# State-space products woven between the projections, with the kernel sums moved ahead

## The chip, the cores and the metric

The kernel runs on one core of a Trainium2 chip. The metric is the device time of one execution, in microseconds (us). The kernel before takes 555.73 us, the median of three runs (555.17 to 556.35). Its one profiled execution took 551.41 us.

The engines are named as in the profile: PE (TensorE, matmul), DVE (VectorE), ACT (ScalarE), POOL (GpSimd) and SP (SyncE, which here only issues DMAs). PSUM has eight banks of 128 x 512 floats, called `bank[0]` to `bank[7]` in the code.

## The reference

Images and text tokens are embedded to h of 32 samples x 68 positions x 256 features. Then come a gated state-space layer (`attn`) and a mixture of four experts with top-2 routing (`ffn`), each added to h. The change lies in the state-space layer:

```python
u = x @ W_x.T + b_x                                  # x: layer norm of h; 512 channels
g = sigmoid(x @ W_g.T + b_g)
u = u * g + conv3(u) * (1 - g)                       # width 3, each channel by itself
dt = clip(softplus(x @ W_dt.T + b_dt).mean(axis=(0, 1)), 0.001, 2.0)      # one number a channel
A = -softplus(A_raw);  A_d = exp(A * dt[:, None]);  B_d = (A_d - 1) / (A + 1e-6) * B_ssm
# scan over the 68 positions: state = A_d * state + B_d * u_t;  y_t = sum_s state * C_ssm
out = y @ W_out.T + b_out
h = h + layernorm(x + out) * ln_g + ln_b
```

Since A_d and B_d don't depend on the position, the scan is a causal convolution: y_t = sum over s of K[t-s] u_s, with a kernel K[k] = sum over the 16 states of B_d C A_d^k, one for each channel. The program computes it that way: for each channel a 68 x 68 Toeplitz matrix of K times the 68 x 32 matrix of u (positions x samples).

## The kernel before, in words

Every engine runs its own instruction list in order, and semaphores join them. The stages that matter:

**A (to about 70 us).** Embedding, layer norm, transposed x (`xT_hi`, `xT_lo`), transposed weights (`WT`). Each projection is done in three matmuls of split parts (hi x hi, hi x lo, lo x hi) by `split3` (lines 392 to 394).

**dt (about 70 to 102 us).** Twenty blocks of x @ W_dt, whose softplus goes from PE to DVE to ACT and back to DVE; DVE then computes `adt` = A * dt (L1279).

**C (about 102 to 189 us), ordered by the list `C_STEPS`.** `("proj", j)` is one chunk of 128 channels, j = 0 to 3. It goes over `NB` = 5 blocks of columns (four of 512, one of 128); a block is 12 matmuls on PE (six for u, six for g), three passes on ACT (`ur` L397, `hb` L1034, `gb` L1041) and four on DVE (L1323 to L1326, which build the mixed u in `hb`). `("turn", j)` transposes the mixed chunk on PE, four samples to a step (L811), through a ring of PSUM banks 4 to 7, and ACT (for the last chunk ACT and DVE in turn) copies it to `U2` (L427). The kernels K are made in between: POOL multiplies the exponents (`Eb`, L596), ACT takes the exponential (L1051), and `kernel_sum(j)` on DVE weighs and sums them (L1309, L1311). `KERNEL_SUMS` puts these sums behind `turn 0`, `turn 1` and the second block of chunk 3. `("kernels",)`, ahead of turn 2, transposes K (L804); DVE copies it to `kt` (L1336, L1338), and SP stores it to `ssm_kernels` (`kpd`) in DRAM (L483).

**Products (about 189 to 251 us).** SP loads the Toeplitz matrices of 32 channels at a time, 16 loads of 680 KB each into three buffers `Tb` (L497; a load waits until the products that read its buffer are done). Load q serves two product steps v = 2q and 2q + 1 of 16 matmuls each (L851; the trace has two records for each matmul), in four column groups of 32 samples. ACT copies the even steps' result to `y` (L966) and DVE the odd ones (L1346), through PSUM banks 0 to 3. In load q, each of the four chunks has eight channels, so all four chunks must be turned before the first product. Beside this SP loads the experts' first weights (`w1raw`, four loads of 512 KB, L503), ACT and DVE split them (`w_hi` L966, `w_lo` L1351), and PE transposes the router's and the output's weights (`BEHIND`, `weights(q)`).

**D (from about 251 us).** Tile by tile: y is transposed (L868), multiplied by `Wo` (L874), added to the residual (L1383), normed, routed (L1428 to L1463) and scattered to the experts' lists; from about 325 us the experts' blocks run beside it, then the combination. The order in D is a sort of steps by the due times in `STARTS` and `AT` (`order(who)`).

Of the kernel before, what the change touches and what calls it, by code (L numbers as in the profile page):

```python
# [23 lines left out]
ALU = mybir.AluOpType  # L24
# [5 lines left out]
def build_kernel(nc, ins, out):  # L30
# [36 lines left out]
    with stack:  # L67
# [66 lines left out]
        ong_b = sb("ong_b", [P, D])  # L134
        onb_b = sb("onb_b", [P, D])
# [22 lines left out]
        def place(start, end, *wanted):  # L158
# [12 lines left out]
        R5 = R4 + size(H * B)  # L171
# [6 lines left out]
        y = at("y", [P, H // HC, L], R1)  # L178
# [15 lines left out]
        ur, hb, gb0 = place(R3, R4, ("ur", [P, 2, N + 2 * B]), ("hb", [P, 2, N]), ("gb0", [P, N]))  # L194
# [4 lines left out]
        (U2,) = place(R4, R5, ("U2", [L, HC, H // HC, B]))  # L199
        h1, x2s, yT, r1, h0r, xb, xg, bT_hi, bT_lo, hn = place(  # L200
            R4, R5, ("h1", [P, NT, D]), ("x2s", [P, NT, DX]), ("yT", [P, 2, HC, P]),
            ("r1", [P, 4, D]), ("h0r", [P, 4, D]), ("xb", [P, 3, D]), ("xg", [P, 4, DX]), ("bT_hi", [P, 2, DC, P], F32R),
            ("bT_lo", [P, 2, DC, P], F32R), ("hn", [P, 2, HF]))
        got_a, got_b, acc = place(R1, R2, ("got_a", [P, 4, D]), ("got_b", [P, 4, D]), ("acc", [P, 4, D]))
# [15 lines left out]
        (kt,) = place(R6, TOP, ("kt", [LR, QN, HC, QH]))  # L220

        (Wor1,) = place(R6, TOP, ("Wor1", [P, H]))
        Wor = [Wor0, Wor1]
# [63 lines left out]
        for k in range(NT + 3):  # L287
# [4 lines left out]
            if k in (NT, NT + 1):  # L292
# [24 lines left out]
                rs=14.6, b3=27.1, c1w=-31.4, c1s=26.7),  # L317
# [3 lines left out]
                table=50.0, rel=47.7, wts=134.7, b1=-14.6, b2=-3.4, rs=4.5, b4=32.1, c1=-1.9, c2=22.3),  # L321
            "odd": dict(yT=21.1, xb=8.8, out=17.5, h0in=6.5, x2T=4.3, lgm=8.1, scat=-0.8, gat=18.4, fin=0.3)}

        def place_of(who, kind, i):

            if kind in BLOCKWISE:
# [9 lines left out]
        def order(who):  # L336

            steps = []
            for kind in AT[who]:
                count = NK if kind in BLOCKWISE else NT if kind in BY_TILE else 2 if kind in BY_PART else len(FB)  # L340
# [4 lines left out]
        C_STEPS = [("proj", 0), ("proj", 1), ("turn", 0), ("proj", 2), ("turn", 1), ("proj", 3), ("kernels",), ("turn", 2),  # L345
                   ("turn", 3)]


        KERNEL_SUMS = {("turn", 0): [0], ("turn", 1): [1, 2], (3, 1): [3]}
# [6 lines left out]
        C_RING = []  # L356
        for step in C_STEPS:
            if step[0] == "kernels":
                C_RING.append(("kT",))
            if step[0] == "turn":  # L360
                C_RING += [("uT", step[1], k) for k in range(B // 4)]

        def c_reader(q):

            if C_RING[q][0] != "uT":
                return "dve"
            _, j, k = C_RING[q]
            return "act" if j < HC - 1 or k % 2 == 0 else "dve"
# [4 lines left out]


        G_RING = [("rw",), ("cbc",), ("wo", 0), ("wo", 1)]

        BEHIND = {15: [0], 19: [1], 29: [2, 3]}
# [40 lines left out]
        def turned(eng, j, who):  # L418

            for k in range(B // 4):  # L420
                q = C_RING.index(("uT", j, k))
                if c_reader(q) != who:
# [1155 lines left out]
```

## Time and profile before

| | |
|---|---|
| median of the runs | 555.73 us |
| profiled execution, its time | 551.41 us |
| profiled execution, its span (first to last instruction) | 549.7 us |
| granted TensorE clock, mean | 0.88 |
| busy: PE / DVE / ACT / POOL | 425.8 / 349.5 / 292.8 / 170.2 us |

The span leaves out 1.71 us of the profiled execution's own time. The page gives busy time as an average over stages with different limits; where a row below has a stretch, that stretch alone is meant. Rows of the timeline read: start, duration, engine, line, operation, output<-input, shapes, and in brackets the idle time ahead of it with what ended it.

### The profile page before, as it was taken

What the parts mean: (1) busy time and instruction counts of PE and PEld (TensorE: products, weight loads), DVE (VectorE), ACT (ScalarE), POOL (GpSimd) and SP (SyncE); (2) the same over time, 40 slices, a digit from 0 to 9 for tenths busy, and PEclk for the clock granted to TensorE, in tenths of its full rate; (3) what the DMA queues carried; (4) which work ended last, traced back from release to release, by engine and by line L of the source; (5) the groups of instructions that cost most, each with busy time, mean ns of one, the idle gap of its engine ahead of it and who ended that gap; (6) DMA issues with size and microseconds to landing.
All of it is one profiled execution on the core that took longest, in us unless ns stands there. A gap on an engine that the chain in (4) does not pass through costs nothing.

```text
span 549.7 us, 10131 instructions
## 1 busy us (share of the span) xinstructions
PE 425.8 (77%) x3078; PEld 352.2 (64%) x3078; DVE 349.5 (64%) x1071; ACT 292.8 (53%) x655; POOL 170.2 (31%) x368
## 2 busy tenths in 40 slices
PE   4999989499893854757888759999897999999100
PEld 2789866388682743646676547878776888887100
DVE  6866578889899200323678876796674466565464
ACT  3754368388982410312543434776674777878121
POOL 2000000500000000001245585577777755655100
PEclk9999999889997765558988969999998999999755
DMA  8961210000000799985111142222224233332342
GB/s 177 217 174 35 63 15 0 1 0 2 0 1 0 173 253 221 202 174 186 47 58 59 58 119 75 59 74 92 79 77 116 69 97 97 98 114 98 124 130 72
DMA packets 51616, 50.97 MB, mean 93 GB/s; under 512 B 25672, under 2 KB 46188, under 8 KB 50156
## 3 DMA queue, kind: packets, MB, share of 16 engines
q1 hardware_dynamic: 47116, 39.70, 30.0%
q0 software_dynamic: 3552, 9.74, 4.8%
q10 hardware_dynamic: 896, 0.89, 0.5%
q8 instruction: 26, 0.43, 0.4%
q14 instruction: 26, 0.21, 0.1%
HBM read 35.56 MB, written 15.81 MB: 93 GB/s over the span
## 4 chain that ended last, share of the span: by engine, by line
PE 44%; DMA 16%; DVE 15%; issue 8%; POOL 8%; ACT 6%; SPq 2%; POOLq 0%; DVEq 0%; ACTq 0%
DMA Tb<-ssm_kernels 9%; PE bank L953 9%; PE bank L392 6%; PE bank L394 5%; PE bank L393 5%; PE bank L874 4%; DMA got_b<-expert_y 3%; POOL expert_y L682 2%; PE bank L851 2%; POOL sorted_x L640 2%; PE bank L943 2%; PE bank L868 1%; DVE hb L1324 1%; PE bank L925 1%; DVE hb L1323 1%
## 5 line engine op out<-in xcount | busy, mean ns | idle before, releaser
L953 PE MATMUL bank<-w,hr 128*128 x320 | 77.9, 387 | 4.4 <-DVE ysb L1535 4.3
L953 PEld LDWEIGHTS bank<-w,hr 128*128 128x128 f32 x320 | 58.8, 194 | 12.6 <-issue 6.0
L1131 ACT ACTIVATE hr<-bank,gsel 128x128 f32<-128x128 f32 x160 | 60.0, 458 | 12.4 <-PE bank L943 12.4
L682 POOL DMA_INDIRECT expert_y<-ysb,toid x40 | 43.4, 1085 | 35.6 <-DVE ysb L1535 24.8
L851 PE MATMUL bank<-Tb,U 68*32 68x68 f32 x1024 | 33.9, 298 | 26.0 <-DMA Tb<-ssm_kernels 24.3
L851 PEld LDWEIGHTS bank<-Tb,U 68*32 68x32 f32 x1024 | 29.4, 144 | 30.1 <-DMA Tb<-ssm_kernels 27.6
L640 POOL DMA_INDIRECT sorted_x<-x2s,slot x34 | 33.5, 986 | 31.1 <-DVE slot L1463 22.6
L874 PE MATMUL bank<-Wo,yT 128*128 128x256 f32 x136 | 38.5, 434 | 2.5 <-ACT yT L966 2.3
L1346 DVE COPY y<-bank 128x272 f32<-128x272 f32 x16 | 7.1, 442 | 50.2 <-PE bank L851 50.2
L1123 ACT ACTIVATE hn<-bank,nmrh,rsh 128x512 f32<-128x512 f32 x40 | 31.1, 777 | 14.5 <-DVE nmrh L1529 12.3
L596 POOL TENSOR_TENSOR Eb<-adt,kio 128x1088 f32<-128x1088 f32 x4 | 8.0, 2027 | 98.4 <-DVE adt L1279 98.4
L1535 DVE COPY ysb<-bank 128x256 f32<-128x256 f32 x40 | 16.9, 421 | 33.4 <-PE bank L953 29.8
L392 PE MATMUL bank<-w_hi,bT_hi 128*128 x80 | 35.0, 437 | 1.5 <-ACT hn L1123 0.8
L616 POOL MEMSET ones<- 2x128 f32 x1 | 0.2, 194 | 110.2 <-PE bank L835 110.2
L966 ACT ACTIVATE y<-bank 128x272 f32<-128x272 f32 x16 | 6.4, 397 | 52.1 <-PE bank L851 52.1
L1520 DVE BATCH_NORM_STATS2 bsth<-bank 128x6 f32<-128x512 f32 x40 | 27.8, 694 | 9.4 <-PE bank L394 9.1
L874 PEld LDWEIGHTS bank<-Wo,yT 128*128 128x128 f32 x136 | 28.4, 220 | 7.4 <-ACT yT L966 3.5
L394 PE MATMUL bank<-w_hi,bT_lo 128*128 x80 | 31.6, 394 | 0.0
L393 PE MATMUL bank<-w_lo,bT_hi 128*128 x80 | 31.3, 391 | 0.0
L943 PE MATMUL bank<-ident,hn 128*128 128x128 f32 x160 | 24.4, 275 | 0.0
L966 ACT ACTIVATE bT_hi<-bank 128x256 fp32r<-128x256 f32 x40 | 15.3, 383 | 16.5 <-PE bank L925 16.2
L427 ACT ACTIVATE U<-bank 68x512 f32<-68x512 f32 x28 | 15.1, 598 | 15.2 <-PE bank L811 15.1
(290 smaller groups left out, 1188.1 us busy)
## 6 DMA issues: line engine op xcount, KB each, us to landing
Tb<-ssm_kernels SPq DMA_DIRECT2D x16, 680.0 KB, 9.4
xg<-sorted_x SPq DMA_DIRECT2D x40, 129.0 KB, 2.1
XI<-in_x_dram SPq DMA_DIRECT2D x12, 288.0 KB, 5.7
h0r<-h_spill SPq DMA_DIRECT2D x17, 128.0 KB, 2.2
got_a<-expert_y SPq DMA_DIRECT2D x17, 128.0 KB, 2.8
got_b<-expert_y SPq DMA_DIRECT2D x17, 128.0 KB, 4.7
out_dram<-acc SPq DMA_DIRECT2D x17, 128.0 KB
w1raw<-in_L_ffn_w_dram SPq DMA_DIRECT2D x4, 512.0 KB, 11.1
```

The lines of the kernel that those rows point to most:

```text
L392: pe.matmul(out_ap, a_hi, b_hi, start=start, stop=False)
L393: pe.matmul(out_ap, a_hi, b_lo, start=False, stop=False)
L394: return pe.matmul(out_ap, a_lo, b_hi, start=False, stop=stop)
L640: pool.indirect_dma_start(xsd[p], bass.IndirectOffsetOnAxis(ap=slot[:, i, n:n + 1], axis=0), x2s[:, i, :], None).then_inc(sem("scattered") ...
L682: pool.indirect_dma_start(yd, bass.IndirectOffsetOnAxis(ap=toid[:, i % 8:i % 8 + 1], axis=0), ysb[:, i % 2, :], None).then_inc(sem(f"y_sto ...
L851: mm = pe.matmul(bank[v % 4][j * B:(j + 1) * B, k * L:(k + 1) * L], U2[:, j, hq, :], Tb[q % 3][0:L, :, j * QH + hq % QH], start=True, stop ...
L874: pe.matmul(ps, yT[:, i % 2, j, :], Wo[:, j, :], start=(j == 0), stop=False)
L943: mm = pe.transpose(bank[3 + i % 2][:, c * P:(c + 1) * P], hn[:, i % 2, c * P:(c + 1) * P], ident[:])
L953: mm = pe.matmul(bank[6][:, 0:D], hr[:, i % 3, c, :], w2[:, bass.ds(expert[i], 1), c, :].rearrange("p o n -> p (o n)"), start=(c == 0), st ...
L1123: act.activation(hn[:, i % 2, :], bank[1 + i % 2][:], ACT.Identity, scale=rsh[:, i % 2:i % 2 + 1], bias=nmrh[:, i % 2:i % 2 + 1]).then_inc ...
L1131: last = act.activation(hr[:, i % 3, c, :], bank[3 + i % 2][:, c * P:(c + 1) * P], ACT.Relu, scale=gsel[:, i, 0, c:c + 1], bias=gsel[:, i, ...
L1520: link(dve.bn_stats(bsth[:, i % 2], bank[1 + i % 2][:]))
```

## The change

- `C_STEPS` is written per column block: `("proj", j, nb)`. The four kernel sums come first on DVE, ahead of all mixing; the transposed kernels (`kT`) follow chunk 0 on PE. Behind chunk 1 and the turn of chunk 0, `woven(2)` and `woven(3)` put two product steps behind each of the first four blocks of chunks 2 and 3. Each product step now needs one chunk only: load q holds 32 neighbouring channels (`quads`), so loads 0 to 3 serve chunk 0, 4 to 7 chunk 1, and so on. The turn of chunk 3 stands between the products of chunk 2 and those of chunk 3.
- The turns' ring has two banks (4, 5) read by ACT and DVE in turn, for every chunk; the products' results have two (6, 7).
- DVE makes the exponents of chunks 0 and 1, POOL those of 2 and 3. Small constants are computed inside the dt loop, at `q == CONSTS_AT` (8).
- One gate buffer `gb` in place of two; `U2` holds two chunks, not four. SBUF is laid out anew.
- `w1raw`, the last norms' vectors and `w2` are loaded from ACT's queue near the end of the products; splitting w1 is a step `w1s` of stage D on ACT and DVE.

```diff
-        KERNEL_SUMS = {("turn", 0): [0], ("turn", 1): [1, 2], (3, 1): [3]}
+        CONSTS_AT = 8
+        SV = 2 * QN // HC
+        turns = lambda j: [("uT", j, k) for k in range(B // 4)]
+        woven = lambda j: [s for nb in range(NB) for s in [("proj", j, nb)] + [
+            ("ssm", SV * (j - 2) + v) for v in range(2 * nb, min(2 * nb + 2, SV))]]
+        C_STEPS = ([("proj", 0, nb) for nb in range(NB)] + [("kT",)] + [("proj", 1, nb) for nb in range(NB)] + turns(0) + [("rw",)]
+                   + woven(2) + turns(1) + [("cbc",)] + woven(3) + turns(2) + [("wo", 0), ("wo", 1)]
+                   + [("ssm", v) for v in range(2 * SV, 3 * SV)] + turns(3) + [("ssm", v) for v in range(3 * SV, 4 * SV)])
...
             for q in range(QN):
                 if q == 0:
                     sp.wait_ge(sem("kernel_sum"), HC)
-                if q == 2:
-                    sp.wait_ge(sem("mixed"), HC * NB)
                 if q >= 3:
                     sp.wait_ge(sem("ssm_mm"), 2 * (q - 2))
...
-            for j in range(HC):
+            for j in range(2, HC):
                 pool.tensor_tensor(Eb[:, j], adt[:, j].rearrange("p (o s) -> p o s", o=1).broadcast_to([P, L, S]),
...
+                if step[0] == "ssm":
+                    v = step[1]
+                    q, j, r = v // 2, v // SV, v % SV
+                    if v % SV == 0:
+                        for who in ("act", "dve"):
+                            last = max(k for k, s in enumerate(C_RING) if s[0:2] == ("uT", j) and c_reader(k) == who)
+                            pe.wait_ge(sem(f"c_read_{who}"), c_read(last)[1])
+                    pe.wait_ge(sem(f"toep_in{q % 3}"), 16 * (q // 3 + 1))
+                    if v >= 2:
+                        pe.wait_ge(sem("y_dve" if v % 2 else "y_act"), (v - 2) // 2 + 1)
...
+                ring = C_RING.index(step)
+                if ring >= 2:
+                    who, n = c_read(ring - 2)
+                    pe.wait_ge(sem(f"c_read_{who}"), n)
+                ps = bank[4 + ring % 2]
...
+            act.wait_ge(sem("conv_consts"), 5)
+            u_parts(0, 0)
+            for j in range(HC):
+                act.wait_ge(sem("exponent" if j < 2 else "exponent_pool"), j % 2 + 1)
+                act.activation(Eb[:, j], Eb[:, j], ACT.Exp).then_inc(sem("powers"), 1)
+                if j == 1:
+                    u_parts(0, 1)
...
+                    if v == 4 * SV - 4:
+                        act.wait_ge(sem("g_mm"), HC * NB)
+                        for e in range(E):
+                            act.dma_start(w1raw[:, e], ins["L0_ffn_w1"][e].rearrange("(c p) h -> p c h", p=P)).then_inc(
+                                sem("experts_in"), 16)
...
+            for j in range(2):
+                dve.tensor_tensor(Eb[:, j], adt[:, j].rearrange("p (o s) -> p o s", o=1).broadcast_to([P, L, S]),
...
+            for j in range(HC):
+                kernel_sum(j)
             for step in C_STEPS:
...
+                elif kind == "w1s":
+                    dve.wait_ge(sem("w1_hi"), i + 1)
+                    dve.tensor_tensor(w1_lo[:, i], w1raw[:, i], w1_hi[:, i].bitcast(F32), ALU.subtract).then_inc(
+                        sem("w1_split"), 1)
```

DVE's list right behind `adt`, in the program before (`nmr`, `nbg`, `ncw`, `vb` are small constants, `hb` rows are the mixing):

```order
L1283 SCALAR_TENSOR_TENSOR nmr<-mv,rs 128x17
L1286 TENSOR_SCALAR nbg<-vec 128x4
L1287 TENSOR_SCALAR ncw<-cw 128x12
L1288 TENSOR_SCALAR ncw<-cw 128x4
L1290 TENSOR_TENSOR vb<-vec,ncw 128x4
L1291 TENSOR_TENSOR vb<-vb,vec 128x4
L1295 MEMSET ur 128x2x32 x2
L1323 SCALAR_TENSOR_TENSOR hb<-ur,ncw,hb 128x480
```

The same place of DVE's list in the changed program (the pair of L1300 and L1302 stands there four times):

```order
L1279 TENSOR_TENSOR adt<-amat,dt 128x64
L1287 TENSOR_TENSOR Eb<-adt,kio 128x1088 x2
L1296 SCALAR_TENSOR_TENSOR wmix<-wmix,winv 128x64
L1297 TENSOR_TENSOR wmix<-wmix,bcs 128x64
L1298 TENSOR_TENSOR wmix<-wmix,bcs 128x64
L1300 TENSOR_TENSOR Eb<-Eb,wmix 128x1088
L1302 TENSOR_REDUCE Kk<-Eb 128x68
```

The two exponents and the four sums have moved ahead of the first mixing row, and the constants have gone from there.

PE's list at the end of stage C and the start of the products, in the program before:

```order
L394 MATMUL bank<-xT_hi,WTg_lo 128x128
L804 MATMUL bank<-ident,Kk 68x128 x4
L811 MATMUL bank<-ident,hb 68x128 x64
L851 MATMUL bank<-Tb_119,U_92 32x68 x32
L851 MATMUL bank<-Tb_120,U_92 32x68 x32
L851 MATMUL bank<-Tb_121,U_92 32x68 x32
```

PE's list in the changed program, from the first block of chunk 2 to the second (the last rows of the one, the product row of 32 matmuls, the first rows of the other):

```order
L384 MATMUL bank<-xT_lo,WTg_hi 128x512
L385 MATMUL bank<-xT_hi,WTg_lo 128x512
L786 MATMUL bank<-Tb_122,U_54 32x68 x32
L383 MATMUL bank<-xT_hi,WTx_hi 128x512
L384 MATMUL bank<-xT_lo,WTx_hi 128x512
```

Where all products stood behind the last turn, each of the first four blocks of chunks 2 and 3 is now followed by the 32 matmuls of one load; eight rows of products are left behind `turn 2`.

DVE's list in stage D of the changed program, at the first `w1s` step:

```order
L1441 TENSOR_REDUCE x2s<-gt 128x2
L1442 CAST slot<-sl 128x2x2
L1495 TENSOR_TENSOR w_lo<-w1raw,w_hi 128x1024
L1375 RECIPROCAL rs<-sd 128x2
L1376 SCALAR_TENSOR_TENSOR r_100<-r_100,mv,lng_b 128x256
```

In the program before, `slot` is followed at once by the reciprocal; the other three `w_lo` rows stand at the same place of the next three pairs of tiles.

## Rows read from the trace of the kernel before

**Rows 1.** The page: what the chain that ended last consists of.

```profile
DMA Tb<-ssm_kernels 9%; PE bank L953 9%; PE bank L392 6%; PE bank L394 5%; PE bank L393 5%; PE bank L874 4%; DMA got_b<-expert_y 3%; POOL expert_y L682 2%; PE bank L851 2%; POOL sorted_x L640 2%; PE bank L943 2%; PE bank L868 1%; DVE hb L1324 1%; PE bank L925 1%; DVE hb L1323 1%
```

**Rows 2.** One stretch: length, busy time (instructions) of each engine, PE clock, DMA, GB/s.

```profile
190.00:220.00 30.00, 15.68 (x488) 13.64 (x477) 3.09 (x7) 3.18 (x8) 0.00 (x0) 0.59 1.02 235
```

**Rows 3.** Timeline of PE, the products of three of the 16 loads.

```profile
189.01 2.07 PE L851 MATMUL bank<-Tb,U 68*32 68x68 f32 x64 [0.98 <-DVE U L427]
...
221.19 2.10 PE L851 MATMUL bank<-Tb,U 68*32 68x68 f32 x64 [0.87 <-DMA Tb<-ssm_kernels]
224.50 2.09 PE L851 MATMUL bank<-Tb,U 68*32 68x68 f32 x64 [1.21 <-DMA Tb<-ssm_kernels]
```

**Rows 4.** The tile Tb: shortest, median and longest time from issue to landing.

```profile
DMA to landing us min/median/max: 6.1/9.4/13.5
```

**Rows 5.** Timeline of DVE behind the dt loop, and of POOL beside it.

```profile
101.95 0.23 DVE L1279 TENSOR_TENSOR adt<-amat,dt 128x64 f32<-128x64 f32 x1
102.25 0.17 DVE L1287 TENSOR_SCALAR ncw<-cw 128x12 f32<-128x12 f32 x1
102.46 1.89 DVE L1288 TENSOR_SCALAR ncw<-cw 128x4 f32<-128x4 f32 x1
104.49 1.84 DVE L1290 TENSOR_TENSOR vb<-vec,ncw 128x4 f32<-128x4 f32 x1
102.27 8.02 POOL L596 TENSOR_TENSOR Eb<-adt,kio 128x1088 f32<-128x1088 f32 x4 [98.42 <-DVE adt L1279]
```

**Rows 6.** Timeline of DVE: a block's mixing starts, chunk 1 ends, and one kernel sum.

```profile
111.95 0.72 DVE L1323 SCALAR_TENSOR_TENSOR hb<-ur,ncw,hb 128x480 f32<-128x480 f32 x1 [3.49 <-ACT gb L1041]
114.73 0.74 DVE L1323 SCALAR_TENSOR_TENSOR hb<-ur,ncw,hb 128x512 f32<-128x512 f32 x1
117.63 0.74 DVE L1323 SCALAR_TENSOR_TENSOR hb<-ur,ncw,hb 128x512 f32<-128x512 f32 x1
137.73 0.33 DVE L1326 TENSOR_TENSOR hb<-ur,hb 128x160 f32<-128x160 f32 x1
157.22 1.28 DVE L1309 TENSOR_TENSOR Eb<-Eb,wmix 128x1088 f32<-128x1088 f32 x1
159.74 1.28 DVE L1309 TENSOR_TENSOR Eb<-Eb,wmix 128x1088 f32<-128x1088 f32 x1
```

**Rows 7.** Timeline of PE: matmuls of a block at half and at full clock, one turn.

```profile
110.92 0.63 PE L394 MATMUL bank<-xT_hi,WTx_lo 128*128 128x512 f32 x1
111.35 0.63 PE L392 MATMUL bank<-xT_hi,WTx_hi 128*128 128x512 f32 x1
114.69 0.40 PE L393 MATMUL bank<-xT_lo,WTx_hi 128*128 128x512 f32 x1
114.92 0.39 PE L394 MATMUL bank<-xT_hi,WTx_lo 128*128 128x512 f32 x1
149.78 3.68 PE L811 MATMUL bank<-ident,hb 128*68 128x128 f32 x32
```

**Rows 8.** Timeline of DVE: copies of the turn and of y.

```profile
187.20 0.69 DVE L427 COPY U<-bank 68x512 f32<-68x512 f32 x1 [0.18 <-PE bank L811]
251.03 0.44 DVE L1346 COPY y<-bank 128x272 f32<-128x272 f32 x1 [3.48 <-PE bank L851]
```

**Rows 9.** Stretches (columns as rows 2) of products alone, for PE's clock.

```profile
189.00:191.00 2.00, 1.99 (x64) 1.80 (x64) 0.00 (x0) 0.40 (x1) 0.00 (x0) 1.00 0.99 226
193.00:196.00 3.00, 2.20 (x76) 1.87 (x68) 0.44 (x1) 0.40 (x1) 0.00 (x0) 0.92 1.12 291
225.00:230.00 5.00, 4.63 (x124) 4.10 (x116) 1.66 (x3) 2.37 (x4) 0.00 (x0) 0.50 1.01 216
```

**Rows 10.** Timeline of DVE: splitting w1, and a wait in stage D.

```profile
244.28 1.21 DVE L1351 TENSOR_TENSOR w_lo<-w1raw,w_hi 128x1024 fp32r<-128x1024 f32 x1
285.15 0.42 DVE L1383 TENSOR_TENSOR r<-bank,xb 128x256 f32<-128x256 f32 x1 [1.32 <-PE bank L878]
```

**Rows 11.** The tile h0r (the residual, read back in stage D): time to landing.

```profile
DMA to landing us min/median/max: 1.9/2.2/3.3
```

More of the change, by code:

```diff
@@ L354, in reached @@
             return max(0, n0 - lag * B), (N if nb == NB - 1 else n0 + w - lag * B)
[L356 to L361, printed above, removed]
         def c_reader(q):
[L365 to L368, printed above, removed]
+            kind = C_RING[q][0]
+            return "act" if kind == "wo" or (kind == "uT" and C_RING[q][2] % 2 == 0) else "dve"
         def c_read(q):
@@ new lines, in _ @@
+                    _, j, nb = step
+                    n0, w = BLOCKS[nb]
+                    c = j * NB + nb
+                    for wt, first, done, read in ((1, 0, "u_mm", "v_init"), (2, 2, "g_mm", "gate")):
+                        if c >= 2:
+                            pe.wait_ge(sem(read), c - 1)
+                        for dc in range(DC):
+                            mm = split3(pe, bank[first + c % 2][:, 0:w], WT[wt][0][:, dc, j * P:(j + 1) * P],
+                                        WT[wt][1][:, dc, j * P:(j + 1) * P], xT_hi[:, dc, n0:n0 + w],
+                                        xT_lo[:, dc, n0:n0 + w], dc == 0, dc == DC - 1)
+                        mm.then_inc(sem(done), 1)
@@ new lines, in _ @@
+                    continue
+                if step[0] == "ssm":
[8 more added lines that the diff above has]
+                        pe.wait_ge(sem("y_dve" if v % 2 else "y_act"), (v - 2) // 2 + 1)
+                    for k in range(4):
+                        h = 4 * r + k
+                        for quad in range(HC):
+                            mm = pe.matmul(bank[6 + v % 2][quad * B:(quad + 1) * B, k * L:(k + 1) * L],
+                                           U2[:, j % 2, HC * h + quad, :], Tb[q % 3][0:L, :, h % QH * HC + quad],
+                                           start=True, stop=True)
+                    mm.then_inc(sem("ssm_mm"), 1)
+                    continue
@@ L817, in _ @@
+                mm.then_inc(sem("c_ps"), 1)
             pe.wait_ge(sem("v_init"), HC * NB)
@@ new lines, in gate @@
+            def gate(j, nb):
+                n0, w = BLOCKS[nb]
+                c = j * NB + nb
+                act.wait_ge(sem("g_mm"), c + 1)
+                if j >= 1:
+                    act.wait_ge(sem("mixed"), NB * (j - 1) + min(nb + 2, NB))
+                act.activation(gb[:, n0:n0 + w], bank[2 + c % 2][:, 0:w], ACT.Sigmoid, bias=nbg[:, j:j + 1],
+                               scale=-1.0).then_inc(sem("gate"), 1)
+            act.wait_ge(sem("adt"), 1)
+            act.activation(wmix[:], adt[:], ACT.Exp).then_inc(sem("a_exp"), 1)
@@ L1344, in _ @@
[L1344 to L1358 removed]
+                    _, j, nb = step
```

395 lines of the change are left out of this document (165 added, 230 removed).

## The prediction

> **What bounds the kernel now.** I read the page's chain first: the largest single item of the chain that ended last is the loading of the Toeplitz matrices, 9% of the span [rows 1]. The stretch in which they arrive shows why: over 30 us the DMA engines are full (1.02) while PE is busy 15.68 us, DVE 3.09 and ACT 3.18, and PE's clock is at 0.59 of full speed [rows 2]. The timeline gives the sizes. One load's products take PE 2.07 to 2.10 us, and PE then waits for the next load; undisturbed loads follow each other every 3.3 us (221.19 to 224.50) [rows 3]. The last result is copied by DVE at 251.03 [rows 8]. So about 62 us, from 189.01 to 251, are a DMA stage with idle engines, whereas in stage C before it DVE works without a gap: a block's four mixing passes take 2.90 us (114.73 to 117.63) [rows 6]. Products beside mixing should then save time. The question is what the kernel sums in front, PE's sum of work and the turns cost.
>
> I work out when the last product ends in the changed kernel, against 251.0 before, and then what stage D adds.
>
> **Until the kernels are summed.** The constants go into the dt loop: some ten small DVE instructions at about 0.2 us (0.17 each plus a gap [rows 5]), 2.3 us in all with the reciprocal. The loop passes work between three engines, so such a stop can be lost whole or be half covered by DVE's own waits; less the 0.45 us of `amat` that leaves the path I take +0.8 us (0 to 2), and `adt` is there at 103.0 instead of 102.2 [rows 5].
>
> Next DVE makes two exponents while POOL makes two. DVE: the trace has no such instruction, but the nearest has the same shape and kind, 1.28 us [rows 6]; POOL: 2.0 us each (8.02 for four) [rows 5]. Side by side that is 4.0 us or less. But rows 5 speak against side by side: while POOL ran its multiplications, DVE instructions on four elements took 1.89 and 1.84 us, where one on 12 elements just before took 0.17. DVE waited out a whole POOL instruction each time. I therefore take all four one after another, 2 x 1.28 + 2 x 2.0 = 6.6 us. (By the Trainium skill, SBUF — State Buffer, "SBUF: two separate sides", a DVE instruction with two SBUF inputs and a GpSimd one that reads SBUF exclude each other for the whole instruction; by that rule it is 6.6, by two independent engines 2.6 ahead of DVE's next step. The trace agrees with it for the four-element rows.) The bounds are 2.6 and 6.6.
>
> Then three small products (0.7 us) and four sums at 2.52 us (157.22 to 159.74 [rows 6]), 10.1 us, with the exponentials on ACT in their shadow. The sums end at 103.0 + 6.6 + 0.7 + 10.1 = 120.4.
>
> **Chunks 0 and 1.** Before, DVE mixed both between 111.95 and 138.06, 26.0 us [rows 6]. The same work, plus 1.2 us for `kt` (memset and copy), ends at 120.4 + 27.2 = 147.6, which is 9.5 us later than before. PE and ACT are long done by then: the kernels cost here what they cost before, but nothing else runs beside them on DVE. The first Toeplitz load is issued at about 127 and lands in 6 to 14 us [rows 4], long before 153, when it is first needed: no cost, with 12 us in hand.
>
> **A turn** is now a relay. With two banks and two readers, DVE reads four of eight steps at 0.69 us [rows 8]; between two of its reads PE must transpose the next step, a quarter of 3.68/2, that is 0.46 us at full clock [rows 7], with two handovers of some 0.2 us. Three rounds of 1.5 us and one read: 5.2 us at full clock, 6.5 at half. DVE is idle for half of it. For chunk 0 I take 6 us: PE begins chunk 2 at 153.5. Later turns are worse placed. PE ends the last small block, DVE is 2.2 us behind with mixing, and only then does it start reading; 7.1 us pass from PE's last block to its next.
>
> **A woven chunk is bound by PE, not by DVE.** Matmuls of 512 columns follow at 0.23 us at full clock [rows 7]: a block is 12 x 0.23 = 2.74 us, the small one 1.34. With 2.1 us of products [rows 3] a block takes PE 4.84 us, against 2.90 + 0.36 on DVE and one 3.3 us load. A chunk: 4 x 4.84 + 1.34 = 20.7 us. The copies of y leave the two result banks in time (DVE has its done 1.6 us before PE wants the bank).
>
> Chunk 2: 153.5 to 174.2. Turn 1: 181.3. Chunk 3: 202.0. Turn 2 and the output weights' transposes: 210.5.
>
> **The tail** is eight loads and a turn. Three loads are in their buffers: 3 x 2.1 us of products, to 216.8. The fourth was issued only when the first of them was done, at 212.8, and needs 6.1 us [rows 4]: 218.9, products to 221. Turn 3, with the clock down: 8 us, 229. Three more buffered: 235.5. The last load, issued at 231.3, lands after 6.1 us and about 1 us of contention with `w1raw`, which starts in those microseconds: 238.4 + 2.1 + 0.6 for handovers = 241.1. **The last product ends at 241.1 instead of 251.0: -9.9 us.**
>
> **Stage D pays some of it back.** Four `w1s` steps come onto DVE at 1.21 us each [rows 10], 4.9 us, and as much as 4 us onto ACT, which is half idle. They were free under the loads. DVE's chain through `slot` is D's own path, with waits like the 1.32 us for PE [rows 10] that can take part of it: 1 to 4.9 us, I take 2. At D's start the 4 MB of `w1raw` and `w2` now lie in front of the first residual tiles, which needed 2.2 us [rows 11]; shared queues could double that: 0 to 3, I take 1.5. And PE enters D with its clock down, where a matmul goes at 0.43 instead of 0.23 us [rows 7]; a few microseconds of D's thin start: +1 (0 to 2). Sum: +4.5.
>
> Together -9.9 + 4.5 = -5.4 us: the profiled execution's 551.41 becomes 546.0, and the median, 4.3 us above it, 555.73 - 5.4 = **550.3 us**. Everything before 70 us and after D is unchanged in content and order.
>
> **Rivals.**
>
> 1. *The clock takes the gain: slower.* PE's clock is at 1.00 at the first products but falls within 193 to 196, after nothing but products since 189; and at 225 to 230 PE is busy 4.63 of 5 us with products at 0.50, without the clock coming back [rows 9]. Products don't hold or raise the clock. Woven, they fill 2.1 of each 4.84 us. If the clock then falls, a block's matmuls take 12 x 0.43 = 5.1 us instead of 2.74, +2.4 us a block; all eight and a half blocks would cost +20 (570), half of them +10 (560). It decides from between two and three slow blocks on. Against it: each block holds 2.7 us of dense full-width matmuls (5.1 when slow), and before, such a stretch brought the clock back between 110.9 and 114.7 [rows 7]; so the fall should mend itself. (By the Trainium skill, TensorE: Matmul & The Clock Gate, "A second HAM failure mode: psum-queue depth-cycling", short idles between groups of matmuls make the clock go to and fro. By that rule the half of the blocks would be slow, 560; no row here shows the mix.)
>
> 2. *The parts hide better than I think.* Exponents side by side (-4), the dt loop without loss (-0.8), D's splitting in DVE's waits (-1), no delay at D's start (-1.5), a turn or two without the 2.2 us lag (-2): 541 to 546. For it: ACT is lightly loaded throughout; against it: rows 5.
>
> 3. *The gain is eaten in D and the turns: no change.* If D pays 4.9 for the splitting and 3 for its start, and the turns go at half clock throughout (+1.3 each): +7 on my sum, 557.
>
> 4. *The change doesn't weave.* If the first products waited for their loads or for y, chunks 2 and 3 would stretch. With loads every 3.3 us against one per 4.84 us and 12 us in hand I see no way to it.
>
> **How the numbers follow.** Mine (546 to 554.5): 0.48. Rival 2: 0.15. Rival 1: 0.22, mostly at 557 to 565. Rival 3: 0.12. Rival 4 and the unforeseen: 0.03. 0.2% of this time, 1.1 us, is about what a measurement can tell from no change. Faster: mine and rival 2, 0.63; within 0.2% (554.6 to 556.8): 0.08, from rival 3 and the mild end of rival 1; slower: 0.29. The range leaves out the extreme of rival 1 and the low end of rival 2: 541 to 563.
>
> **What would show it.** In the profile after: kernel sums on DVE ending near 120; the exponents' instructions on DVE and POOL stretched or not; the first products near 156, spaced 4.8 us, with a load landed before each; PE's clock near 1.00 between 155 and 200 (near 0.7, rival 1 holds); turns of about 7 us of which PE is idle a part; the last product near 241; DVE's `w_lo` in D followed by later copies. If products begin before 150 or PE waits for loads in chunks 2 and 3, my sum is wrong.

## The result, and the profile after

| | before | after |
|---|---|---|
| median of the runs | 555.45 us (554.7 to 556.35, 4 runs) | 562.69 us (560.7 to 564.58, 4 runs) |
| profiled execution, its time / its span | 551.41 / 549.7 us | 563.82 / 562.1 us |
| granted TensorE clock, mean | 0.880 | 0.899 |
| busy: PE / DVE / ACT / POOL | 425.8 / 349.5 / 292.8 / 170.2 us | 451.9 / 355.8 / 285.7 / 169.7 us |

The ratio is 1.0114, with a 95% interval of 1.0071 to 1.0158: the changed kernel is slower. 550.3 was forecast, between 541 and 563. PE was busy 26 us longer, although it was to do the same matmuls. Ratios here and below compare fast runs alone, those within 1.5% of the kernel's fastest, while medians are of all runs, so that a difference can come out a little otherwise by the two.

The rows of after, in the order of the sum in the prediction. First DVE behind the dt loop and POOL beside it, timeline (against [rows 5, 6]):

```profile
104.65 0.22 DVE L1279 TENSOR_TENSOR adt<-amat,dt 128x64 f32<-128x64 f32 x1
105.00 6.17 DVE L1287 TENSOR_TENSOR Eb<-adt,kio 128x1088 f32<-128x1088 f32 x2
111.10 0.21 DVE L1296 SCALAR_TENSOR_TENSOR wmix<-wmix,winv 128x64 f32<-128x64 f32 x1
...
120.75 1.29 DVE L1302 TENSOR_REDUCE Kk<-Eb 128x68 f32<-128x1088 f32 x1
121.95 0.71 DVE L1313 SCALAR_TENSOR_TENSOR hb<-ur,ncw,hb 128x480 f32<-128x480 f32 x1
...
149.82 0.32 DVE L1316 TENSOR_TENSOR hb<-ur,hb 128x160 f32<-128x160 f32 x1
```

```profile
104.95 5.08 POOL L575 TENSOR_TENSOR Eb<-adt,kio 128x1088 f32<-128x1088 f32 x2 [101.04 <-DVE adt L1279]
```

The exponents cost DVE 6.1 us in all, from 105.00 to 111.10, and not 2.6: the two engines did take turns. The sums end at 121.95, chunks 0 and 1 at 150.14 (forecast 120.4 and 147.6).

Next PE, timeline: the products of one woven block with the projection's matmul on either side, and those of the tail (against [rows 3]):

```profile
158.35 0.39 PE L385 MATMUL bank<-xT_hi,WTg_lo 128*128 128x512 f32 x1
158.67 3.06 PE L786 MATMUL bank<-Tb,U 68*32 68x68 f32 x64
161.66 0.50 PE L383 MATMUL bank<-xT_hi,WTx_hi 128*128 128x512 f32 x1
...
220.46 7.73 PE L786 MATMUL bank<-Tb,U 68*32 68x68 f32 x192
228.36 3.08 PE L786 MATMUL bank<-Tb,U 68*32 68x68 f32 x64 [0.17 <-DMA Tb<-ssm_kernels]
231.38 1.09 PE L806 MATMUL bank<-ident,hb 128*68 128x128 f32 x8
...
237.60 10.95 PE L786 MATMUL bank<-Tb,U 68*32 68x68 f32 x256 [0.83 <-issue]
```

The first products begin at 158.67; 156.2 was forecast. But one load's products (x64) take 3.06 us, not 2.07 to 2.10, and blocks follow each other every 5.9 us (158.67, 164.60), not every 4.84. Three loads take 7.73 us in the tail, four take 10.95.

The stretches of the weave, of the tail and of D's start, with the columns of [rows 2]:

```profile
155.00:190.00 35.00, 33.18 (x368) 26.95 (x367) 18.35 (x35) 14.36 (x26) 0.00 (x0) 0.99 0.31 81
190.00:220.00 30.00, 27.88 (x344) 22.67 (x343) 16.89 (x28) 12.84 (x23) 0.00 (x0) 1.00 0.36 95
220.00:250.00 30.00, 27.73 (x554) 24.72 (x554) 6.28 (x12) 6.29 (x14) 0.87 (x6) 1.00 0.64 165
250.00:260.00 10.00, 3.80 (x17) 2.76 (x16) 2.21 (x5) 1.68 (x3) 0.72 (x1) 0.89 1.01 338
260.00:270.00 10.00, 8.96 (x27) 6.45 (x26) 2.15 (x8) 3.75 (x6) 1.45 (x2) 0.59 0.06 20
```

The weave does what it was to do: the DMA engines, full before (1.02 in [rows 2]), are at 0.31 to 0.36, and a load lands in 4.9 us (median) rather than 9.4 [rows 4]. PE's clock is 1.00, and PE, now the bound, hardly waits. So it is PE's own work that grew. All the matmuls of the products, grouped by shape (instructions | busy us, mean ns of one record), before and after:

```profile
L851 PE MATMUL bank<-Tb,U 68*32 68x68 f32 x1024 | 33.9, 298 | 26.0 <-DMA Tb<-ssm_kernels 24.3 <-DVE U L427 1.0 <-issue 0.7
```

```profile
L786 PE MATMUL bank<-Tb,U 68*32 68x68 f32 x1024 | 46.2, 362 | 1.1 <-issue 0.8 <-DMA Tb<-ssm_kernels 0.2
```

24.3 us of waiting for loads went, and 12.3 us of busy time came, for the same number, shape and type of matmuls. (A record overlaps its neighbours of the other column groups, so that busy time is less than count times mean.) The clock is not the reason: before, a load's products took 2.07 us at a clock of 1.00 (189.01) and 2.09 at 0.50 (224.50) [rows 3, 9]; here they take 3.06 at 1.00. Most of the rest of PE's 26 us is elsewhere: the matmuls of the output projection in stage D (L846, before L874) were busy 44.2 us against 38.5, those of the dt loop 49.0 against 45.3, both while the clock was lower than before (see below).

Last, the start of stage D, from the chain of waits of after (start, length, what), against [rows 8] for the last copy of y:

```profile
248.67 0.34 SPq L498
...
249.65 0.58 SPq L501
250.23 0.06 issue
250.28 5.83 DMA hr<-in_L_attn_b_out_dram
256.11 0.02 issue
256.13 0.58 DVE bo_hl L1350
```

The last y copy starts at 248.61 on DVE (before: 251.03). The bias of the output projection, 2 x 1 KB, is issued on SP's queue at 249.65, after the 4 MB of weights that ACT's queue issues from 244.3 to 248.7, and lands 5.8 us later; the first residual sum starts at 258.7 (before: 256.5). The last copy was 2.4 us earlier, and the first sum 2.2 us later. After that PE's clock is 0.59 for 10 us (before: 1.00). The first expert's load `xg` is issued at 336.1 instead of 324.7: 11.4 of the 12.4 us between the two spans are there by then. How they add up: -2.4 at the last y copy, +4.6 from there to the first residual sum, +9.2 from this sum to `xg`. The last of these stretches, before and after (columns of [rows 2]):

```profile
256.52:324.73 68.21, 53.79 (x265) 41.66 (x265) 50.89 (x213) 30.63 (x66) 33.32 (x45) 0.90 0.27 84
258.70:336.08 77.38, 62.85 (x265) 47.65 (x265) 54.28 (x216) 34.10 (x70) 36.79 (x47) 0.76 0.20 61
```

PE does the same 265 matmuls in it, at a clock of 0.76 rather than 0.90. So two things have to be explained: products that cost PE 12.3 us more and leave the last copy only 2.4 us earlier, and a stage D that is 13.8 us longer up to `xg`.

### The profile page after: what moved, and what is told of

The parts are those of the page before. It is cut to its first block, busy times and chain, and to the rows that moved or that the text cites. A ratio compares the mean times of both kernels' runs of the same rounds, so it can differ in the third digit from the quotient of the medians.

```text
span 562.1 us, 10159 instructions
## 1 busy us (share of the span) xinstructions
PE 451.9 (80%) x3078; PEld 369.0 (66%) x3078; DVE 355.8 (63%) x1085; ACT 285.7 (51%) x641; POOL 169.7 (30%) x366
## 4 chain that ended last, share of the span: by engine, by line
PE 48%; DVE 17%; DMA 10%; issue 8%; POOL 8%; ACT 5%; SPq 3%; POOLq 0%; DVEq 0%; ACTq 0%
PE bank L925 7%; PE bank L383 6%; PE bank L846 6%; PE bank L786 5%; PE bank L384 5%; PE bank L385 5%; DMA got_b<-expert_y 3%; POOL expert_y L661 2%; PE bank L806 2%; POOL sorted_x L618 2%; DMA Tb<-ssm_kernels 2%; PE bank L915 2%; DVE hb L1314 1%; DVE hb L1313 1%; PE bank L840 1%
## 5 line engine op out<-in xcount | busy, mean ns | idle before, releaser
L786 PE MATMUL bank<-Tb,U 68*32 68x68 f32 x1024 | 46.2, 362 | 1.1 <-issue 0.8
L618 POOL DMA_INDIRECT sorted_x<-x2s,slot x34 | 36.3, 1067 | 34.6 <-DVE slot L1442 26.1
L846 PE MATMUL bank<-Wo,yT 128*128 128x256 f32 x136 | 44.2, 482 | 2.5 <-ACT yT L938 2.3
L786 PEld LDWEIGHTS bank<-Tb,U 68*32 68x32 f32 x1024 | 41.5, 140 | 5.2 <-issue 2.8
L846 PEld LDWEIGHTS bank<-Wo,yT 128*128 128x128 f32 x136 | 31.7, 245 | 8.7 <-ACT yT L938 3.3
L575 POOL TENSOR_TENSOR Eb<-adt,kio 128x1088 f32<-128x1088 f32 x2 | 5.1, 2556 | 101.0 <-DVE adt L1279 101.0
L806 PE MATMUL bank<-ident,hb 128*68 128x128 f32 x128 | 20.4, 303 | 15.8 <-DVE U L420 13.5
L806 PEld LDWEIGHTS bank<-ident,hb 128*68 128x68 f32 x128 | 14.4, 144 | 21.1 <-DVE U L420 16.5
L1313 DVE SCALAR_TENSOR_TENSOR hb<-ur,ncw,hb 128x512 f32<-128x512 f32 (+2 forms) x20 | 13.4, 668 | 23.4 <-ACT gb L1009 23.2
L388 ACT ACTIVATE ur<-bank,vec 128x512 f32<-128x512 f32 (+1 forms) x20 | 12.4, 622 | 26.0 <-PE bank L385 22.5
```

The costliest lines, as they stand in the source:

```text
L618: pool.indirect_dma_start(xsd[p], bass.IndirectOffsetOnAxis(ap=slot[:, i, n:n + 1], axis=0), x2s[:, i, :], None).then_inc(sem("scattered") ...
L786: mm = pe.matmul(bank[6 + v % 2][quad * B:(quad + 1) * B, k * L:(k + 1) * L], U2[:, j % 2, HC * h + quad, :], Tb[q % 3][0:L, :, h % QH * H ...
L806: mm = pe.transpose(ps[0:L, (b % 4) * P:(b % 4 + 1) * P], hb[:, j % 2, :].rearrange("p (t b) -> p t b", b=B)[:, :, b], ident[:])
L846: pe.matmul(ps, yT[:, i % 2, j, :], Wo[:, j, :], start=(j == 0), stop=False)
```

## Experiments

Theory A: the product matmuls are slower because of which floats they read. Four column groups of PE run side by side, one for each `j` before and each `quad` after. Before, they read columns 8 floats apart in a row of `Tb` (`j * QH`); regrouped by neighbouring channels, they read four neighbouring floats. Rival U: it is the stationary operand, whose four rows of `U2` are now neighbours too. Rival B: two result banks rather than four. Rival C: what runs beside the products, or right before them on PE. Theory D: the weights' loads hold up stage D. The code cuts below leave out the semaphore waits, except where the wait is what changes.

**e1_tb8**: the changed kernel with another order of channels inside `Tb`.

```diff
-  dve.tensor_copy(kt[0:L].rearrange("k q c -> k (q c)"), bank[4 + q % 2][0:L, :])
+  dve.tensor_copy(kt[0:L].rearrange("k q (a m) -> k q m a", a=HC),
+                  bank[4 + q % 2][0:L, :].rearrange("k (q m a) -> k q m a", a=HC, m=QH))
-  Tb[q % 3][0:L, :, h % QH * HC + quad]
+  Tb[q % 3][0:L, :, quad * QH + h % QH]
```

> The changed kernel, with the channels of a load in the order of before inside the Toeplitz buffers: the copy to kt permutes them, and the four column groups of a product read columns of Tb that lie 8 floats apart, as in the kernel before, in place of 4 neighbouring ones. U2, the banks, the order of the work and the result are those of the changed kernel. Theory A (the groups run at one time, and reading neighbouring floats of Tb slows them): 32 matmuls take 2.1 us again and not 3.05, PE's busy time falls by about 12 us, the time by 8 to 12 us, to about 552. Rival B (two result banks are too few) and rival C (the projections' matmuls or the mixing beside them slow the products): 3.05 us as in the changed kernel and 562.5 us. Rival U (it is the neighbouring rows of U2): the same, no change.

Measured: 552.29 us (median of 10 runs; ratio to before 0.9922, 0.9883 to 0.9961). That is 10.4 us less than the changed kernel by the medians (10.7 by the ratios, 1.0114 - 0.9922 of 555.45), and faster than the one before. The products of the first two woven blocks on PE, and the group of all of them:

```profile
158.89 2.07 PE L786 MATMUL bank<-Tb,U 68*32 68x68 f32 x64
...
163.88 2.07 PE L786 MATMUL bank<-Tb,U 68*32 68x68 f32 x64
```

```profile
L786 PE MATMUL bank<-Tb,U 68*32 68x68 f32 x1024 | 33.3, 295 | 3.6 <-issue 2.1 <-DMA Tb<-ssm_kernels 1.5
```

Nothing else in PE's list is different, and the first products begin at the same time within 0.3 us. Busy time is back at 33.3 us; the last product starts at 239.1 rather than 248.2. Theory A holds. Rivals U, B and C each expected no change here, since rows of `U2`, banks and order are those of the changed kernel.

**e2_u8**: the changed kernel with the other operand's neighbours taken apart. It pairs kernels and values of different channels.

```diff
-  U2[:, j % 2, HC * h + quad, :]
+  U2[:, j % 2, h // QH * QC + quad * QH + h % QH, :]
```

> The changed kernel, with only the stationary operand's place changed: the four column groups take rows of U2 that lie 8 channels (1 KB) apart, not neighbouring ones. Tb is read as in the changed kernel, so that the products pair the kernels of one channel with the values of another. Theory A (neighbouring floats of Tb): 32 matmuls still take 3.05 us, the time stays at 562. Rival U (neighbouring rows of U2): 2.1 us, the time about 552. Rivals B and C: 3.05 us.

Measured: 562.54 us (one run), products:

```profile
L786 PE MATMUL bank<-Tb,U 68*32 68x68 f32 x1024 | 46.2, 362 | 1.0 <-issue 0.8
```

To the tenth what they were. Rival U is out: time and products are those of the changed kernel.

**e3_before_tb1** puts the neighbouring floats into the kernel before; **e4_before_2bank** gives that kernel two result banks. The edits, each alone:

```diff
-  Tb[q % 3][0:L, :, j * QH + hq % QH]
+  Tb[q % 3][0:L, :, hq % QH * HC + j]
```

```diff
-  if v >= 4: pe.wait_ge(sem("y_dve" if v % 2 else "y_act"), (v - 4) // 2 + 1)
+  if v >= 2: pe.wait_ge(sem("y_dve" if v % 2 else "y_act"), (v - 2) // 2 + 1)
-  bank[v % 4]
+  bank[v % 2]
```

> The kernel before, in which the four column groups read neighbouring floats of Tb (columns 4m, 4m+1, 4m+2, 4m+3 of a load, not m, m+8, m+16, m+24); each chunk's values so meet the kernels of other channels of the load. Theory A: 32 matmuls of L851 take about 3.05 us in place of 2.07 to 2.10, also where nothing runs beside them; a load takes 6.1 us in place of 4.2, which the transfers (6 to 13 us each, one behind the other) partly hide: the time grows by 2 to 12 us. Rivals U, B and C: 2.1 us and 555.7 us.

> The kernel before, with two result banks for the products in place of four (v % 2, and the wait for the copy of the step before the last). Rival B (with two banks the matmuls take longer): 32 matmuls take about 3 us. Theory A and rivals U and C: 2.1 us each, with short waits for the y copies between steps (up to 0.5 us each, hidden where PE waits for a load): 555.7 to 558 us.

Measured: e3 559.92 us, e4 556.66 us (one run each). The groups of products in e3, then in e4:

```profile
L851 PE MATMUL bank<-Tb,U 68*32 68x68 f32 x1024 | 47.3, 365 | 15.8 <-DMA Tb<-ssm_kernels 11.5 <-issue 3.3 <-DVE U L427 1.0
```

```profile
L851 PE MATMUL bank<-Tb,U 68*32 68x68 f32 x1024 | 33.6, 298 | 25.8 <-DMA Tb<-ssm_kernels 23.7 <-issue 1.1 <-DVE U L427 1.0
```

The slow products of e3 appear in the old order of work as well, with four banks and no projection beside them; two banks change nothing. Rivals B and C are out as the cause of the slow products. e3 also shows what hides the cost: 13.4 us more of busy time take 10.2 us from PE's waits ahead of the products (26.0 to 15.8).

**e11_before_tb1** is e3's kernel again, timed.

> e3_before_tb1 once more, now timed: the kernel before with the four column groups on neighbouring floats of Tb (the products pair kernels and values of different channels). Its matmuls took 13.4 us more in all (47.3 against 33.9). Where products stand in the shadow of the Toeplitz loads, most of that is hidden: the theory expects 1 to 4 us more than before, ratio 1.002 to 1.007. The rival, that the order of before would lose as much by it as the changed one (10 us, the distance from the changed kernel to e1_tb8), expects 1.015 to 1.02.

Measured: 559.71 us against 555.98 for before, ratio 1.0042 (0.9992 to 1.0092). Much the same addition to PE's work, 12.3 and 13.4 us, costs 10.7 us by the ratios (10.4 by the medians) where PE is the bound, and 2.3 us by the ratio (-0.4 to 5.1 by its interval, 3.7 by the medians) behind the loads. The rival's 1.015 lies outside the interval, and the ratio of the two medians, 1.0067, doesn't reach it either.

**e8_tb4** and **e9_tb2** ask how far apart is enough: the changed kernel with the groups 4 and 2 floats apart (`h % QH // 4 * 16 + quad * 4 + h % 4`, and the same with 2 and 8). Both pair kernels and values of different channels.

> The changed kernel, in which the four column groups read columns of Tb that lie 4 floats (16 bytes) apart; the products so pair kernels of one channel with values of another. Neighbouring floats gave 3.05 us for 32 matmuls, 8 floats apart 2.07 us. If only reads of the same floats' neighbourhood of 16 bytes disturb one another: 2.07 us and about 552 us. If it is 32 bytes or more: 3.05 us, or something between, and 557 to 562 us.

> As e8_tb4, with the four column groups 2 floats (8 bytes) apart. If the disturbance falls off by pairs: between 2.07 and 3.05 us for 32 matmuls. If it holds within 16 bytes or more: 3.05 us and 562 us.

Measured, one run each: 550.49 us at 4 floats, 551.32 us at 2. The tile `Tb` on PE (shortest, median, longest ns of one; first and last start) of after, e9, e8 and e1:

```profile
L786 PE MATMUL bank<-Tb,U x1024: 275/372/404, 158.7 to 248.2; 68*32 68x68 f32 x171
```

```profile
L786 PE MATMUL bank<-Tb,U x1024: 277/315/331, 157.9 to 241.0; 68*32 68x68 f32 x171
```

```profile
L786 PE MATMUL bank<-Tb,U x1024: 279/296/323, 157.0 to 237.9; 68*32 68x68 f32 x171
```

```profile
L786 PE MATMUL bank<-Tb,U x1024: 274/295/323, 158.9 to 239.1; 68*32 68x68 f32 x171
```

A median of 372 ns at a distance of 1 float, 315 at 2, 296 at 4, 295 at 8: at 16 bytes (4 floats) the groups disturb one another no more than at 32. My second expectation for e9, that the disturbance holds within 16 bytes, was wrong: at 8 bytes 20 of the 77 ns are left.

**e5_loads**: e1_tb8 with its weights' loads spread.

```diff
-  if v == 4 * SV - 4:
-      for e in range(E):
+  if v in (18, 20, 22, 24):
+      for e in [(v - 18) // 2]:
           act.dma_start(w1raw[:, e], ...)
+  if v == 26:
+      for t, name in ((ong_b, ...), (onb_b, ...)):
+          act.dma_start(t[:], ...)
-  act.dma_start(w2[:], ...)     # behind the last y copy, as the norms' two
+  if i == 3:                    # SP, kind "h0in"
+      sp.dma_start(w2[:], ...)
```

> e1_tb8 (552.3 us), with its loads placed otherwise: the four loads of w1raw go out one by one behind the y copies 18, 20, 22 and 24, the norms' vectors behind copy 26, and w2 (2 MB) from SP's queue behind the fourth load of h0r, as before the change. Theory D (stage D starts late because the residual's loads stand behind 4 MB of weights): in e1_tb8 the last y copy ends at 239.9 and the first residual sum starts at 248.9, 9.0 us later, against 5.5 before the change; here 5 to 6 us, and PE, which idles less, keeps the full clock for the first output steps, 2 more us: 546 to 549 us. Rival (the loads are only moved: beside the last products' Toeplitz loads they make PE wait as much as they did in front of D, and D's start is set by something else): 551 to 553 us.

Measured: 548.83 us (ratio 0.9882, 0.9831 to 0.9933), 3.5 us less than e1_tb8 by the medians and 2.2 by the ratios, whose intervals overlap. This is the upper end of what theory D expected, and by the times alone it isn't certain. The traces show what moved. DVE at D's start, in e1_tb8 and in e5_loads:

```profile
239.48 0.44 DVE L1346 COPY y<-bank 128x272 f32<-128x272 f32 x1 [3.99 <-PE bank L786]
246.24 0.28 DVE L1351 CAST bo_hl<-hr 2x256 fp32r<-2x256 f32 x1 [6.32 <-DMA hr<-in_L_attn_b_out_dram]
...
248.88 0.42 DVE L1363 TENSOR_TENSOR r<-bank,xb 128x256 f32<-128x256 f32 x1 [0.67 <-PE bank L850]
254.44 0.42 DVE L1363 TENSOR_TENSOR r<-bank,xb 128x256 f32<-128x256 f32 x1 [5.14 <-PE bank L850]
```

```profile
242.08 0.44 DVE L1349 COPY y<-bank 128x272 f32<-128x272 f32 x1 [3.99 <-PE bank L789]
244.80 0.28 DVE L1354 CAST bo_hl<-hr 2x256 fp32r<-2x256 f32 x1 [2.28 <-DMA hr<-in_L_attn_b_out_dram]
...
248.00 0.42 DVE L1366 TENSOR_TENSOR r<-bank,xb 128x256 f32<-128x256 f32 x1 [1.13 <-PE bank L853]
251.30 0.42 DVE L1366 TENSOR_TENSOR r<-bank,xb 128x256 f32<-128x256 f32 x1 [2.88 <-PE bank L853]
```

From the last y copy to the first residual sum it is 5.9 us rather than 9.4 (start to start; before the change 5.5), and to the second sum 9.2 rather than 15.0, as PE's clock is 1.00 in 250 to 260, not 0.78. But the last y copy is 2.6 us later: the loads now stand among the Toeplitz loads. The theory and its rival both had a part: 5.8 us won up to the second sum, 2.6 of them given back ahead of it.

**e6_splits**: e5_loads with `w1s` out of stage D.

```diff
-  ... E if kind == "w1s" else ...              # count of steps in order(who)
+  ... 0 if kind == "w1s" else ...
-  if v in (18, 20, 22, 24):                    # w1raw's loads
+  if v in (16, 18, 20, 22):
+  if v >= 24:                                  # ACT, behind the even y copies
+      copy(w1_hi[:, (v - 24) // 2], w1raw[:, (v - 24) // 2])
+  if v >= 25:                                  # DVE, behind the odd y copies; i = (v - 25) // 2
+      dve.tensor_tensor(w1_lo[:, i], w1raw[:, i], w1_hi[:, i].bitcast(F32), ALU.subtract)
```

> e5_loads, with w1raw two steps earlier still (copies 16 to 22) and its splitting taken out of stage D: ACT rounds one expert behind each of the y copies 24, 26, 28, 30 (1.05 us each), DVE subtracts behind 25, 27, 29, 31 (1.22 us each). Theory W (stage D is bound through PE, DVE and ACT in turn, so that 4.9 us of DVE and 4.2 us of ACT in its way cost some of their length): 1 to 3 us less than e5_loads. Rival (they fill idle time of DVE in D, and here the last of them stands in front of the first residual sum): the same as e5_loads within 0.5 us, or up to 1.2 us more.

Measured: 547.07 us (ratio 0.9853, 0.9810 to 0.9896), 1.8 us less by the medians, 1.6 by the ratios; the intervals overlap, so that the size is uncertain. The traces agree with it: from the first residual sum to the first `xg` load it is 68.8 us (247.8 to 316.6), against 71.1 in e5_loads (248.0 to 319.1). In the tail, though, a new wait came up, in PE's waits (line, releaser: total, times, longest us) between 205 and 245:

```profile
PE bank L789 <- ACT y L941: 4.5, 1, 4.5
PE bank L789 <- issue: 2.2, 2, 1.4
PE bank L789 <- DMA Tb<-ssm_kernels: 2.1, 2, 1.8
```

ACT stood before the first split until 236.84, for `w1raw`, with its y copy behind it. And in 205 to 215 the DMA engines were nearly idle (second to last column), with all three buffers of `Tb` full, before they were overloaded:

```profile
205.00:215.00 10.00, 8.04 (x161) 7.01 (x163) 3.64 (x7) 3.76 (x7) 0.00 (x0) 1.00 0.20 54
215.00:225.00 10.00, 7.76 (x159) 6.33 (x151) 2.70 (x5) 2.22 (x5) 0.00 (x0) 0.83 1.04 273
```

**e10_gap**: e6_splits with the four loads of `w1raw` put into that gap, on SP's queue.

```diff
   sp.dma_start(Tb[q % 3]...)
+  if q == 10:
+      sp.wait_ge(sem("g_mm"), HC * NB)
+      for e in range(E): sp.dma_start(w1raw[:, e], ...)
```

> e6_splits (547.1 us), with the four loads of w1raw issued by SP right behind Toeplitz load 10, as soon as the last projection is done, not behind y copies on ACT's queue. In e6_splits the DMA engines idled from about 205 to 213 us (the Tb buffers were full), then carried w1raw beside the Toeplitz loads up to 236; ACT waited 7.6 us for w1raw, and PE 4.5 us of it for ACT's y copy and 7.5 us in all behind late Toeplitz loads. Theory G (2 MB fit into that gap at the 250 GB/s of the neighbouring stretches, in 8 us): w1raw lands by 215, the splits wait for nothing, the last product ends about 4 to 6 us earlier, 541.5 to 544 us. Rival (load 11 queues behind them and PE waits for it instead, or the half clock in turn 3 decides): within 1.5 us of e6_splits.

Measured: 543.06 us (median of 6 runs; ratio to before 0.9776, 0.9735 to 0.9818), 4.0 us less than e6_splits by the medians and 4.3 by the ratios, whose intervals just touch. PE's waits in the same stretch, and the gap:

```profile
PE bank L814 <- DVE U L420: 2.2, 5, 1.0
PE bank L794 <- DMA Tb<-ssm_kernels: 2.1, 2, 1.1
PE bank L794 <- issue: 2.0, 2, 1.2
PE bank L848 <- DVE y L1353: 0.6, 1, 0.6
```

```profile
205.00:215.00 10.00, 7.80 (x92) 6.53 (x95) 5.70 (x11) 4.60 (x9) 0.00 (x0) 1.00 0.86 282
```

`w1raw` is issued from 206.1, each load lands within 7.0 us, and the wait for ACT is gone: theory G holds. The two traces differ by only 0.4 us at the first `xg` load (316.2 and 316.6), because e10's execution wrote `adt` 2.65 us later than e6's (the dip of the clock told below); counted from `adt`, it is 211.0 us against 214.0. This kernel takes 12.9 us less than the one before by the medians (12.4 by the ratio), and 18.8 by the ratios to 19.6 by the medians less than the changed one.

## Why the prediction was wrong

**The number.** 562.69 lies just inside the range of 541 to 563, among the values that the prediction gave to rival 1, a falling clock in the weave. That rival did not happen, so that the range holds the result by luck. The forecast itself, faster by 5.4 us, was wrong in sign.

**The step that failed is the duration of a product.** "With 2.1 us of products [rows 3] a block takes PE 4.84 us", and the same 2.1 us went into the eight loads of the tail. The 2.1 us were read from a kernel in which the operands lie otherwise, and carried over. Regrouping the loads was costed only as a change of what a product must wait for; that it changes which floats of `Tb` are read at one time, in a line that the diff shows, was not looked at. It measured 3.06 us a load in the weave (3.08 and 2.6 to 2.7 in the tail), 12.3 us of busy time in all, and 10.4 us of the kernel's time (e1_tb8). With that one term put right the kernel stands at 552.3 (551.1 by the ratio), 1 to 2 us from the forecast, and the sign is the one predicted.

That closeness is in part luck, for two sizes were off the other way round. From the end of `adt` to the end of the products the forecast was 138.1 us (103.0 to 241.1); e1_tb8 took 134.7 (104.8 to 239.5). And stage D was to add 4.5 us; from the last y copy to the end of the span it is 298.7 us before and 308.1 in e1_tb8, 9.4 more (against e4, which is before's kernel but for two banks, and has 301.4, it is 6.7).

**Stage D was the second miss, its start first.** I took 1.5 us for the 4 MB ahead of the residual tiles, from 0 to 3. From the last y copy's start to the first residual sum's start it was 5.5 us before and 10.1 after: +4.6. It wasn't the residual tile itself that came last, but the bias issued behind it. In e5_loads the same distance is 5.9.

Behind the first residual sum, D's size was off too. From this sum to the first `xg` load it is 68.2 us before (70.0 in e4) and 77.4 after, 73.8 in e1_tb8, 71.1 in e5_loads, 68.8 in e6_splits. The stretch of e1_tb8:

```profile
248.88:322.68 73.80, 59.26 (x265) 44.93 (x265) 55.00 (x215) 33.89 (x70) 36.60 (x47) 0.82 0.22 66
```

Its clock is 0.82, against 0.90 before and 0.76 after. So e1_tb8's 5.6 us over before are the late second sum (2.3), the splitting (2.3 between e5 and e6) and about 1 us more. The changed kernel needs 3.6 us more again, for the same instructions in D. All five traces with the changed kernel's stage D show this: from the last y copy to the end it is 313.5 and 313.3 us with the slow products (after, e2), 308.1, 310.6 and 308.2 without (e1, e8, e9). Why D runs at a lower clock behind slow products no experiment shows.

**The clock.** Rival 1 is wrong: the clock was 0.99 and 1.00 through the whole weave and the tail. Its ground, "Products don't hold or raise the clock", was read from stretches in which PE waited for loads between products; in the tail of after, four loads' products in a row (237.60 to 248.55) ran at 1.00. In e1_tb8, with shorter products, PE waits for loads between the tail's products again (1.5 us in two waits, and 2.1 us in two more for which the trace names nothing), and the clock there is 0.83 (215 to 235) and 0.66 (235 to 245). (The Trainium skill's "psum-queue depth-cycling" in TensorE: Matmul & The Clock Gate, weighed in the prediction, asks for short idles; PE had next to none here (busy 33.18 of 35 us in 155 to 190), so this trace doesn't test it.) After's clock fell where PE had idled for 5.42 us, in D's first output steps, as term three of stage D had it: eight matmuls of L846 took 3.62 us there against 1.89 before, and the second residual sum came 5.6 us behind the first instead of 3.3. The forecast said +1 (0 to 2); that one step alone was +2.3.

**What was right.** The exponents: 6.6 us forecast one after another, 6.1 measured, and two independent engines would have had 2.6 (this is the place where the Trainium skill's page SBUF — State Buffer, "SBUF: two separate sides", was weighed; the trace agrees with it, at 6.17 us for two DVE instructions beside 5.08 us for two of POOL). The sums: 10.1 forecast, 10.1 measured. Chunks 0 and 1: 27.2 forecast, 28.2 measured. The turns: about 7 us forecast from block to block, 6.6 measured (180.85 to 187.43). No waits for loads in the weave. In e1_tb8 the last y copy starts at 239.48; 241.1 was forecast for the last product's end. The splitting in D: 2 us forecast, 1.6 to 1.8 measured by the times (within overlapping intervals), 2.3 in the traces.

**The constants** look wrong at first, and aren't: `adt` is written at 104.65 after and 101.95 before, +2.7 us where +0.8 was forecast. But in that execution the clock was 0.85 and 0.81 in 70 to 90, and 1.00 in before's profile. This dip is there in some executions, whichever kernel: e3, e4 and e11, with before's loop, had it and wrote `adt` at 105.1, 105.4 and 104.6; e2, e5, e8 and e9, with after's loop, didn't have it and wrote `adt` at 102.9, 103.2, 102.6 and 103.2; e1 and e10, with after's loop and the dip, at 104.5 and 105.2. At like clocks the difference is +0.7 to +1.2 without the dip, and -0.9 to +0.6 with it. Of the 12.4 us between the two spans 1.5 to 2 are therefore no part of the change; the 7.2 us between the medians are the better measure of it.

The bookkeeping, by the ratios: -4.3 us from before to e1_tb8 (weave, sums, turns and all of stage D together), +10.7 for the neighbouring floats, +6.3 in all. Of what stage D had to pay in e1_tb8, e5 and e6 took back 3.8 by the ratios (5.2 by the medians).

What stays open: whether the disturbance comes from the reads in the same cycle or from ones close behind each other, since the distance alone was varied, and why it was less in the tail (2.6 to 2.7 us a load) than in the weave and in the load at 228.36 (3.06 to 3.08); and why stage D is 3 to 5 us longer behind the slow products.

## What to carry to other kernels

A duration read from a trace belongs to an access pattern as well as to a shape: when a regrouping changes which addresses neighbouring column groups of PE read, it has to be priced anew, and in the source it is an index, not an instruction. A cost that hid behind a bound comes into the open when the change removes that bound: the same slow matmuls cost 2 to 4 us behind the loads and 10 where nothing hid them. When loads are moved, look for the stretch in which the DMA engines idle because all buffers are full, and for the kilobyte that everything waits for behind the megabytes.

## What the runs showed of the hardware that had not been expected

- Four column groups of 32 columns, each a product of 68 x 32 by 68 x 68 in f32, with moving operands in strides of 32 floats: a record takes 295 ns (median) if the groups' operands lie 8 floats apart, 296 at 4, 315 at 2, 372 at 1. The distance of the stationary operands (128 bytes or 1 KB) makes no difference (362 ns mean in both).
- These products don't follow PE's clock: 2.07 us a load at 1.00 and 2.09 at 0.50 in the kernel before.
- Two result banks in place of four cost these products nothing (298 ns mean in both).
- PE's clock can differ between executions of the same part: 1.00 throughout, or 0.77 to 0.83 in 80 to 90 us, with `adt` written 2.7 to 3.5 us later with before's loop and 1.4 to 2.6 with after's (e6, at 0.90, lost nothing). One profile for each kernel can't tell a difference of that size.
